# Order of the last routing steps, of the expert weights in SyncE's queue, and the attention's reciprocals in a two-layer kernel

## The reference

```
x += selective_scan(norm(x))      # 256 channels x 64 states, along the 1024 tokens, then out_proj
x += moe(norm(x))                 # 8 experts, each token picks 2, at most 640 tokens an expert:
                                  #   relu(t @ w1[e]) @ w2[e], 256 -> 1024 -> 256, times the gate
x += linear_attention(norm(x))    # 16 heads of 16
x += (silu(x @ w_gate) * (x @ w_up)) @ w_down     # 256 -> 1024 -> 256, on norm(x)
```

```
KV   = sum_n K[n, d] * V[n, e]          Ksum = sum_n K[n, d]
Z[n] = 1 / (Q[n] . Ksum + 1e-6)         out[n] = (Q[n] @ KV) * Z[n]
```

## Time and profile before

| what | us |
|---|---|
| median of three runs | 1322.31 |
| the three runs | 1314.65, 1322.31, 1324.99 |
| the profiled execution | 1319.23 |
| its span | 1317.8 |
| PE busy | 1105.0 |
| DVE busy | 842.5 |

### The profile page before, as it was taken

The page is one execution under the profiler, slowest core; times in us unless marked ns, Lnnn a source line. Parts: engine busy times, 40 slices in busy tenths (PEclk is TensorE's granted clock), DMA queues, the critical chain, the costliest instruction groups (busy, mean ns, idle before and its releaser), DMA issues.

```text
span 1317.8 us, 29499 instructions
## 1 busy us (share of the span) xinstructions
PE 1105.0 (84%) x11952; PEld 701.6 (53%) x11952; DVE 842.5 (64%) x1006; ACT 503.4 (38%) x1245; POOL 306.7 (23%) x930
## 2 busy tenths in 40 slices
PE   3647888878878898888873799999999588999998
PEld 2435444444544454444432578888887245475565
DVE  5858999999999999999992111111211577742211
ACT  3865556566656655566551111111111110122110
POOL 9741222222233222522242011111111200000000
PEclk9865789999999899999996799999999698999999
DMA  3897345543222222322223823222200400000000
GB/s 107 243 281 215 77 96 132 131 118 82 57 62 76 55 60 52 82 57 49 53 70 148 313 79 102 100 101 99 80 16 16 128 0 0 0 9 8 16 16 16
DMA packets 171687, 112.02 MB, mean 85 GB/s; under 512 B 93637, under 2 KB 162248, under 8 KB 169248
## 3 DMA queue, kind: packets, MB, share of 16 engines
q1 hardware_dynamic: 163120, 88.69, 24.2%
q0 software_dynamic: 8000, 20.87, 4.8%
q10 hardware_dynamic: 432, 0.59, 0.2%
HBM read 63.18 MB, written 45.90 MB: 83 GB/s over the span
## 4 chain that ended last, share of the span: by engine, by line
PE 47%; DVE 27%; issue 14%; SPq 5%; ACT 4%; DMA 2%; POOL 1%; DVEq 0%; ACTq 0%; POOLq 0%
DVE h L1161 19%; PE psum L1412 11%; PE psum L1424 11%; PE psum L1896 8%; PE psum L1907 4%; PE psum L945 3%; DVE den L1726 2%; PE psum L931 2%; PE psum L1852 2%; ACT decay L1046 1%; PE psum L912 1%; SPq L278 1%; SPq L199 1%; PE psum L1844 1%; SPq L282 1%
## 5 line engine op out<-in xcount | busy, mean ns | idle before, releaser
L1161 DVE TENSOR_TENSOR_SCAN h<-decay,psum 128x1024 f32<-128x1024 f32 x256 | 565.8, 2268 | 14.8 <-ACT psum L1056 9.0
L1046 ACT ACTIVATE decay<-psum 128x512 f32<-128x512 f32 x512 | 279.2, 600 | 200.5 <-PE psum L912 197.9
L931 PE MATMUL psum<-xdiag,bstat 96*128 96x64 bf16 x4096 | 176.4, 200 | 56.2 <-DVE h L1161 53.4
L931 PEld LDWEIGHTS psum<-xdiag,bstat 96*128 96x128 bf16 x4096 | 144.9, 102 | 82.0 <-DVE h L1161 73.5
L912 PEld LDWEIGHTS psum<-rows,shared 32*128 32x128 bf16 x4096 | 79.0, 96 | 183.4 <-issue 119.9
L945 PE MATMUL psum<-h,cstat 128*32 128x512 f32 x1024 | 150.2, 664 | 1.1 <-DVE h L1161 1.1
L1412 PE MATMUL psum<-xdt,shared 128*128 128x320 f32 x512 | 141.0, 436 | 0.7 <-ACT xdt L1471 0.7
L1424 PE MATMUL psum<-shared,hid 128*128 128x256 f32 x640 | 139.5, 379 | 0.6 <-ACT hid L1465 0.6
L1317 POOL TENSOR_TENSOR carry<-decay,h 128x16 f32<-128x16 f32 x240 | 57.9, 241 | 343.7 <-ACT decay L1046 343.4
L1424 PEld LDWEIGHTS psum<-shared,hid 128*128 128x128 f32 x640 | 121.0, 190 | 17.2 <-issue 1.1
L912 PE MATMUL psum<-rows,shared 32*128 32x64 bf16 x4096 | 110.5, 195 | 15.7 <-ACT decay L1046 7.4
(11 more groups left out here) (201 smaller groups left out, 1100.9 us busy)
## 6 DMA issues: line engine op xcount, KB each, us to landing
shared<-in_w SPq DMA_DIRECT2D x16, 1024.0 KB, 4.8
xdiag<-x_parts_d SPq DMA_DIRECT2D x256, 48.0 KB
x_parts_d<-x_parts POOLq DMA_DIRECT2D x46, 256.0 KB, 7.8
parts_d<-dt_parts SPq DMA_DIRECT2D x24, 256.0 KB, 8.4
rows<-parts_d SPq DMA_DIRECT2D x128, 48.0 KB
disp_d<-zero SPq DMA_DIRECT2D x4, 1305.0 KB, 8.5
xd<-disp_d SPq DMA_DIRECT2D x8, 652.5 KB, 6.4
picked_d<-zero SPq DMA_DIRECT2D x4, 1024.0 KB, 5.2
```

The source lines that it names most:

```text
L931: ins = pe.q.matmul(to.rearrange("p d (s e) -> p s d e", e=2), bstat[0:ROWS, c % 2, b, :], xdiag[0:ROWS, c % 2, b, :, d, :], start=True, s ...
L1046: act.q.activation(decay[:, gi % NB, 8 * half:8 * half + 8, :], per_d(bank_a[half]), ACT.Exp).then_inc(sem("exp"), 1)
L1161: dve.q.tensor_tensor_scan(out=h[:, half_slot(c, half), ch:ch + G, :].rearrange("p d t -> p (d t)"), data0=decay[:, gi % NB, :, :].rearran ...
```

## The change

Three things are edited. In SP's queue "load_experts" moves from the last group of the scan to behind y_sel of chunk 30. In the tail of the list, b3's turn, scores, CHOOSE (without exp) and rank move ahead of the residual of tile 15, its scores ahead of the projection of tile 15; b3's exp follows b4's NORM; b3's WEIGH, SETTLE, count and scatters come ahead of all of b4's CHOOSE. In the second layer den is made once per head: kden has 8 used columns of 32, the four quarters q of a block's 512 tokens go to four strips of 32 partitions, so that den is one 128x256 tile for both halves; DVE adds and takes one reciprocal a block; PE then spreads the result with c_sel, a 0/1 matrix (256 KB, loaded with the other weights), to the product "rec" of 128x512 a half, which ACT copies to SBUF, and DVE multiplies as before. num is unchanged. PE does den, num, rec in this order for a block.

```diff
@@ scan_schedule
-        if gi == TOTAL - 1:
-            yield ("load_experts",)
 ...
     yield ("y_sel", CHUNKS - 2)
+    yield ("load_experts",)
     yield from ((name, b3) for name in NORM)
     for js in (js for js in Y_STEPS if js):
         yield ("y", CHUNKS - 1, js)
+    yield ("turn", b3)
     yield ("y_out", CHUNKS - 1)
+    yield ("turned", b3)
     yield stamp("yT", TILES - 1)
-    yield ("turn", b3)
     yield stamp("yt", TILES - 1)
-    yield ("turned", b3)
+    yield from (("score", b3, i) for i in range(ROUTED[b3][1]))
     yield stamp("proj", TILES - 1)
     yield stamp("proj2", TILES - 1)
-    yield from (("score", b3, i) for i in range(ROUTED[b3][1]))
+    yield from ((name, b3) for name in CHOOSE if name != "exp")
+    yield ("rank", b3)
     yield stamp("resid", TILES - 1)
     yield from ((name, b4) for name in NORM)
+    yield ("exp", b3)
     yield from (("turn", b4), ("turned", b4), ("score", b4, 0))
-    yield from ((name, b3) for name in CHOOSE)
-    yield ("rank", b3)
-    yield from ((name, b4) for name in CHOOSE[:-1])
-    yield from ((name, b3) for name in WEIGH)
-    yield from ((name, b3) for name in (*SETTLE, "count"))
+    yield from ((name, b3) for name in (*WEIGH, *SETTLE, "count"))
     yield from (("scatter", b3, i, j) for i in range(ROUTED[b3][1]) for j in range(2))
-    yield (CHOOSE[-1], b4)
+    yield from ((name, b4) for name in CHOOSE)
     yield ("rank", b4)
@@ rest
-                   c_mask=sb("mask", [P, P]),
+                   c_mask=sb("mask", [P, P]), c_sel=sb("sel", [P, 4, P]),
@@ second_products
-            yield from ((kind, x, hh) for hh in range(2) for kind in ("den", "num"))
+            yield ("den", x)
+            yield from ((kind, x, hh) for kind in ("num", "rec") for hh in range(2))
@@ second_layer
-    kden = sb("kden", [P, 2, P])
-    den = sb("den", [P, 2, 512])
+    kden = sb("kden", [P, 2, 32])
+    den, rec = sb("den", [P, 2 * P]), sb("rec", [P, 2, 512])
@@ second_layer, on_dve
+        dve.q.memset(kden[:, :, :], 0.0).then_inc(own.sem, own.up())
+        dve.wait_ge(own.sem, own.n)
 ...
-                ins = dve.q.tensor_scalar(kden[:, hh, :], mask[:, :], bank_kv[hh][:, P:P + 1], None, ALU.mult)
+                ins = dve.q.tensor_scalar(kden[:, hh, 0:P // DK], mask[:, 0:P:DK], bank_kv[hh][:, P:P + 1], None, ALU.mult)
 ...
         def attend(blk):
+            kd = ("den", blk)
+            dve.wait_ge(*table.is_full(kd))
+            if blk:
+                dve.wait_ge(*table.is_full(("rec", blk - 1, 1)))
+            dve.q.tensor_scalar(den[:, :], table.bank(kd)[:, 0:2 * P], 1e-6, None, ALU.add).then_inc(*table.evacs(kd))
+            dve.wait_ge(*table.is_evac(kd))
+            dve.q.reciprocal(den[:, :], den[:, :]).then_inc(sem("den_inv"), 1)
             for hh in range(2):
-                kd, kn = ("den", blk, hh), ("num", blk, hh)
-                dve.wait_ge(*table.is_full(kd))
-                dve.q.tensor_scalar(den[:, hh, :], table.bank(kd)[:, :], 1e-6, None, ALU.add).then_inc(*table.evacs(kd))
-                dve.wait_ge(*table.is_evac(kd))
-                dve.q.reciprocal(den[:, hh, :], den[:, hh, :]).then_inc(own.sem, own.up())
-                dve.wait_ge(own.sem, own.n)
+                kn = ("num", blk, hh)
                 dve.wait_ge(*table.is_full(kn))
+                dve.wait_ge(*table.is_evac(("rec", blk, hh)))
 ...
-                dve.q.tensor_tensor(at[:, blk % 2, hh, :], table.bank(kn)[:, :], den[:, hh, :], ALU.mult
+                dve.q.tensor_tensor(at[:, blk % 2, hh, :], table.bank(kn)[:, :], rec[:, hh, :], ALU.mult
                                     ).then_inc(*table.evacs(kn))
@@ second_layer, on_act
+            elif step == "attend":
+                for hh in range(2):
+                    key = ("rec", x, hh)
+                    act.wait_ge(*table.is_full(key))
+                    if x:
+                        act.wait_ge(*table.is_evac(("num", x - 1, hh)))
+                    act.q.copy(rec[:, hh, :], table.bank(key)[:, :]).then_inc(*table.evacs(key))
@@ second_layer, on_pe, attend (den and num of a half in turn before)
+            pe.wait_ge(sem("q_decayed"), 2 * blk + 2)
+            kd = ("den", blk)
+            pe.wait_ge(*table.is_free(kd))
             for hh in range(2):
+                for q in range(4):
+                    ins = pe.q.matmul(table.bank(kd)[32 * q:32 * q + 32, P * hh:P * hh + P], kden[:, hh, :],
+                                      qt[:, hh, 512 * blk + P * q:512 * blk + P * q + P], start=True, stop=True)
+            ins.then_inc(*table.fulls(kd))
+            for hh in range(2):
+                key = ("num", blk, hh)
+                pe.wait_ge(*table.is_free(key))
+                pe.q.matmul(table.bank(key)[:, :], bd[:, hh, :], qt[:, hh, t5], start=True, stop=True).then_inc(*table.fulls(key))
+            for hh in range(2):
+                key = ("rec", blk, hh)
+                pe.wait_ge(*table.is_free(key))
+                pe.wait_ge(sem("den_inv"), blk + 1)
+                for q in range(4):
+                    ins = pe.q.matmul(table.bank(key)[:, P * q:P * q + P], sel[:, q, :], den[:, P * hh:P * hh + P],
+                                      start=True, stop=True)
+                ins.then_inc(*table.fulls(key))
@@ lay_out
+        "c_sel": (np.arange(P)[:, None, None] == 32 * np.arange(4)[:, None] + head).astype(np.float32),
```

More of the change, by code:

```diff
@@ L1607, in second_layer @@
     ident, eps = s["ident"], s["eps"]
-    wq, wkv, wo, brow, dec_row, dec_col, mask, wgu, wd = wts.values()
+    wq, wkv, wo, brow, dec_row, dec_col, mask, sel, wgu, wd = wts.values()
     xb = sb("xb", [P, TILES, D])
```

## The result

| | before | changed | ratio, 95% interval |
|---|---|---|---|
| median (lowest to highest), us | 1321.91 (1314.65 to 1324.99), 4 runs | 1305.82 (1303.11 to 1309.03), 4 runs | 0.9882 [0.985, 0.9913] |
| profiled execution, us | 1319.23, span 1317.8 | 1303.11, span 1301.5 | |

The medians differ by 16.1 us, the two profiled spans by 16.3. I forecast 13.6, and 1305.6 for the profiled execution.

What follows compares the result with a forecast made beforehand. DVE bounds the scan, PE the experts and last blocks; the change touches two places where PE waits. Gains of 9.2 + 4.4 = 13.6 us from 1319.23 gave 1305.6, own range 1302 to 1309, whole range 1299 to 1315.

Steps and rivals of the forecast that it cites:

- y_sb behind the weights: Turn from scan to experts: small y_sel loads wait behind 4 x 1024 KB of weights; moved ahead, land at 696.6, not 703.07.
- rival C: Turn: small loads stay late, not held by the weights or queue order not kept; reordering gains 2.9 us; 1311.9; chance 0.12.
- the low bound: Turn: y_sel data land 1.3 us after their issue ends, as in an ordinary chunk; the forecast took 2.0 us.
- parts 1 and 2: Turn: weights' issue moved behind y_sel, and tiles 12 to 14 routed first; 9.2 us together, bounds 7.5 and 10.3.
- the walk: Turn: step-by-step timing of the reordered tail with PE at full clock, first scatter at 706.7, 9.4 us earlier.
- The order of the tail: Turn: tiles 12 to 14 chosen and scattered before tile 15's choice, same instructions reordered; 2.9 us if small loads stay late.
- Covers: Turn: b4's slots ready about 5 us before their scatter is due, weights 16 us before expert 0 wants them.
- Part 3: Second layer's attention: reciprocals once per head, 4.4 us gained; 7.1 without the fall of the clock.
- The clock in block 1: Second layer's attention: 5.7 us of PE idle time before rec lets the clock fall, costing 2.7 us.
- Rival B: Second layer's attention: clock holds or block 1 is better filled, gain there 7.1 us; total 16.3, 1302.9; chance 0.16.
- Rival A: Second layer's attention: PE is the bound, new matmuls and waits eat DVE's saving, no gain there; 1310; chance 0.22.
- Rival D: Second layer's attention: four PE waits for DVE each drop the clock, 3.3 us each; slower, 1320.9; chance 0.06.

Runs made afterwards that it cites:

- the order alone: Kernel before with only the new order of the tail, the weights' issue still ahead of y_sel: 1316.02 us, ratio 0.9986.
- the warm kernel: Changed kernel plus six overwritten 512-column products in PE's idle time before rec of block 1: 1302.93 us, ratio 0.9862 against the kernel before.
- exp first: Changed kernel with exp, weights and scatters of tiles 12 to 14 ahead of tile 15's norm: 1300.43 us, ratio 0.9852 against the kernel before.

## Why the prediction was right

- **y_sb behind the weights.** Right, and rival C falls: with nothing ahead it landed 1.3 us after the end of its issue, with 4 MB ahead it was read 6.4 to 7.4 us later than that. I had taken 2.0; the low bound was the truth. This 0.7 us is the mis-sized term of parts 1 and 2. y_sel's issue to first scatter was to be 14.5 and was 13.5 us; the walk behind it held within 1 us at each step (the choice of b3 was done and the residual of tile 15 began 8.0 us after y_sel's issue instead of 8.9; from there to the scatter 5.44 instead of 5.6). The four matmuls of the last projection took 1.13 us instead of the 1.88 of the earlier trace rows, so the clock was up by then, as the walk had it.
- **The order of the tail.** Right, but a small part: 1.0 to 1.2 us alone, counted from PE's read of y_sb, and 1.2 to 1.6 on top of the queue (13.46 against 14.62 and 15.04). The only price that the prediction gave it by itself, 2.9 us in rival C, was too high. It took the walk at full clock, but behind a late y_sb PE comes back at half: the projection took 2.05 us in the order alone and 1.13 in the changed kernel.
- **Covers.** b4's slots had 5.9 us instead of the 5 counted, the weights were never waited for, the eight scatters ran 1.29 apart, and the experts began at 719.97 and ran on as a whole (0.31 us; 0.12 of it is the narrower kden, 1.58 us from the last product K x V to den instead of 1.70).
- **Part 3, 4.4 us, was 3.6.** The gain of block 0 up to block 1's add was 1.17 us instead of 1.3; the prediction's own terms (2.3 to 2.6 less 0.6 and 0.8) give 0.9 to 1.2, not the 1.1 to 1.3 written there. The start of qkv 3 came 2.45 us earlier (2.7). From the heads to the end of gate_up 0 it was 38.25 us (37.8), where 0.45 of the missing 0.8 us lies. The mis-sized terms are the passes: rec is 2.02 us a block to its last end instead of 1.7. In block 0 the next product starts 1.86 us after rec's first pass, 0.116 us for a pass of 128 columns, not a quarter of the 0.43 of 512 columns. den is 0.57 to 0.68 us instead of 0.5, so four do run at a time. The reciprocal of 128x256 took 1.75 us, as worked out by width.
- **The clock in block 1.** The fall was forecast at 2.7 us and is 2.40, by the warm kernel. Rival B needed it not to happen, and it did in every profile of the unaltered kernel. Rival A falls by the stage: 3.6 us, repeated.
- **Rival D** did not come about, but my argument against it was wrong: that the clock had held behind a wait of 2.3 us in block 0. It held in three of six profiles and fell in the other three, 1.8 us each. What kept D away is that the new attention has no such wait except in block 1: elsewhere PE waits 0.51 to 1.19 us, and the clock was 1.00. Part of what part 3 gives is this: against the old stage in its worse half of profiles it is 5.4 us.
- **The drain.** The drain at a change of the tiling mode that the Trainium skill states (TensorEngine Tiling (Array Packing), Key Properties), weighed in the prediction at 2.2 us in all, can be bounded now. Ahead of den (32 rows of output), 0.64 us pass from the last product K x V to den in block 1 of the changed kernel, and 0.55 in the kernel before, whose den is of full size. den itself takes 0.57 us up to num, where 0.46 would be a quarter of the y passes' 0.114 each. Behind it the four passes of num take 1.98 us; four passes of the same width behind others of full size take 1.88 (1104.78 in the timeline of the changed kernel). All differences together are 0.3 us a block and 1.2 in all, so the changes of mode cost at most half of the 2.2 us that I had allowed. How much of the 0.3 is a drain isn't shown.
- **The sum.** 9.2 + 4.4 became 10.4 + 3.6. That 13.6 met 14.05 is in part luck, as two errors of opposite sign, +1.2 and -0.8, nearly cancel. The last 2.2 us of the 16.3 are 1.9 of the scan and 0.3 of the experts, which the forecast put at nothing; they are why the profiled execution took 1303.11 and not the 1305.6 forecast. The median of 1305.82 lies closer to that figure only by chance: the median of before was itself 2.7 us above the profiled execution from which I counted.

## What to carry to other kernels

Small loads that are on the path go ahead of big ones in the same queue, and the big one's own due time is the only price: here 4 MB moved back cost nothing that the traces show and gave 8.5 to 9.3 us, where the reordered routing gave 1 to 2 and the rewritten attention 4. When an engine is relieved, look at what the other one does in the gap that is left: behind PE's idle 5.4 us its clock cost another 2.4 us, and dummy products in the gap gave these back though nothing started sooner. Cut the span at events that both traces have, and compare stage by stage: the stages of the changed kernel repeat to 0.1 us, medians of the same kernel against before only to several us. Look for a second profile of the old kernel too: two of its stages differed by 0.8 and 1.8 us between profiles.

## What the runs showed of the hardware

- The clock behind a wait is no fixed price. In the old attention it fell behind 1.87 us in six profiles of six, and behind 2.3 us in three of the same six. In the new one it fell in block 1 behind 3.7 and 5.4 us in every profile, and behind the waits of 0.5 to 1.2 us in none. A single profile that shows it held is no evidence that it will.
- When it falls, it is paid by what PE does next: 1.70 us on rec and 0.61 on ao 0 in block 1, nothing in the old gate_up 0, where PE had to wait for DVE anyway.
- A table load of ACT (1.28 us) started as soon as ACT's program reached it, not when the data were there: in exp first at 696.90 (the copy before it ends at 696.89), for data of 698.94. Put before that wait it cost nothing; in the changed kernel, behind b4's square root, it lies on the path.
- Passes of 128 columns with new weights each take 0.116 us where a quarter of a 512-column pass is 0.108; the 32-row products at four places 0.036 to 0.042 each.
